# A filter bias written by ScalarE before the products, in place of a bias product behind them, in a two-layer graph kernel

## What is computed

```python
def layer0(features, edge_distances, ...):                 # bf2 is a filter bias
    h = features @ W_lin.T
    basis = gaussian_smearing(edge_distances)               # 50 columns
    ef = shifted_softplus(basis @ Wf1 + bf1) @ Wf2 + bf2    # the filter, 128 per edge
    messages = h[senders] * ef
    agg = segment_sum(messages, receivers)
    return shifted_softplus(agg @ Wm1 + bm1) @ Wm2 + bm2

def layer1(node_feats, edge_vec, edge_length, ...):         # mlp_b2 is a filter bias
    emb = radial_embedding(edge_length)                     # 8 columns
    h = silu(emb @ mlp_w0 + mlp_b0)
    h = silu(h @ mlp_w1 + mlp_b1)
    w = (h @ mlp_w2 + mlp_b2).reshape(-1, 4, 32)            # the filter
    # four products of w with the gathered features and the edge's direction,
    # then segment_sum per receiver and an output product

x = layernorm(x + layer0(x, edge_weight, ..., src, dst))
x = layernorm(x + layer1(x, edge_attr_3, edge_weight, src, dst, ...))
```

## Time and profile before

| | |
|---|---|
| time, median of 3 executions | 2209.0 us (2207.32 to 2209.87) |
| time of the profiled execution | 2202.79 us |
| span of the profiled execution | 2201.0 us |
| TensorE busy | 1899.1 us (86%) |
| VectorE busy | 1370.4 us (62%) |
| ScalarE busy | 637.9 us (29%) |
| GpSimd busy | 1569.6 us (71%) |
| mean granted TensorE clock | 0.823 of 2.4 GHz |

### The profile page before, as it was taken

The page is one execution under the profiler, slowest core; times in us unless marked ns, Lnnn a source line. Parts: engine busy times, 40 slices in busy tenths (PEclk is TensorE's granted clock), DMA queues, the critical chain, the costliest instruction groups (busy, mean ns, idle before and its releaser), DMA issues.

```text
span 2201.0 us, 34359 instructions
## 1 busy us (share of the span) xinstructions
PE 1899.1 (86%) x10138; PEld 1431.4 (65%) x10138; DVE 1370.4 (62%) x2905; ACT 637.9 (29%) x995; POOL 1569.6 (71%) x1599
## 2 busy tenths in 40 slices
PE   5887877778777887777879999999999999899997
PEld 4665666666666666666557777666776676677766
DVE  6755555555555555555645776666667666666665
ACT  3643343343433433432541111111111111111114
POOL 4777777777777777777147777777777777777770
PEclk8777777777777777777867998898999998988889
DMA  7422222222222222222021111111121221111112
GB/s 217 126 78 78 76 81 76 76 81 76 76 81 76 80 76 76 81 76 62 6 82 51 55 54 53 53 54 54 53 55 54 54 55 54 52 55 54 53 52 66
DMA packets 105683, 152.31 MB, mean 69 GB/s; under 512 B 33982, under 2 KB 65490, under 8 KB 105546
## 3 DMA queue, kind: packets, MB, share of 16 engines
q0 software_dynamic: 50656, 103.11, 17.3%
q1 hardware_dynamic: 54652, 46.76, 7.0%
q10 hardware_dynamic: 336, 2.01, 0.3%
HBM read 138.53 MB, written 13.21 MB: 69 GB/s over the span
## 4 chain that ended last, share of the span: by engine, by line
POOL 68%; issue 22%; PE 7%; DMA 1%; DVE 1%; ACT 1%; SPq 0%; POOLq 0%; DVEq 0%; ACTq 0%
POOL sent L436 68%; DMA unit_in<-in_x 1%; PE bank L984 1%; PE bank L800 1%; PE bank L767 1%; PE bank L815 1%; PE bank L953 1%; PE bank L759 1%; PE bank L988 0%; PE bank L942 0%; PE bank L871 0%; PE bank L879 0%; PE bank L802 0%; DMA sent<-up_table,senders 0%; DMA sent<-h_table,senders 0%
## 5 line engine op out<-in xcount | busy, mean ns | idle before, releaser
L436 POOL DMA_INDIRECT sent<-up_table,senders x784 | 775.3, 989 | 268.2 <-issue 237.7
L436 POOL DMA_INDIRECT sent<-h_table,senders x784 | 766.5, 978 | 263.9 <-issue 238.6
L815 PE MATMUL bank<-onehot,msg 128*128 128x128 f32 x4704 | 794.0, 332 | 7.1 <-DVE sums L1098 4.2
L815 PEld LDWEIGHTS bank<-onehot,msg 128*128 128x128 f32 x4704 | 706.4, 235 | 116.0 <-issue 91.4
L800 PE MATMUL bank<-Wf_sb,hid 128*128 128x128 f32 x1568 | 281.1, 334 | 94.8 <-DVE hid L1114 94.5
L1124 DVE TENSOR_TENSOR msg<-bank,sent 128x512 f32<-128x512 f32 x196 | 135.6, 692 | 349.1 <-issue 189.7
L800 PEld LDWEIGHTS bank<-Wf_sb,hid 128*128 128x128 f32 x1568 | 246.0, 239 | 153.5 <-DVE hid L1114 100.2
L800 PEld LDWEIGHTS bank<-w_sb,h 64*128 64x128 f32 x1568 | 195.5, 193 | 213.1 <-issue 116.2
L631 ACT ACTIVATE soft<-soft 128x512 f32<-128x512 f32 (+1 forms) x209 | 131.2, 628 | 591.2 <-DVE soft L1105 558.4
L1085 DVE TENSOR_TENSOR onehot<-relT,iota 128x512 f32<-128x512 f32 x392 | 268.8, 686 | 39.3 <-PE bank L815 37.1
L800 PE MATMUL bank<-w_sb,h 64*128 64x128 f32 x1568 | 233.9, 291 | 47.3 <-DVE msg L1157 46.4
(11 more groups left out here) (133 smaller groups left out, 1330.4 us busy)
## 6 DMA issues: line engine op xcount, KB each, us to landing
basis<-in_edge_weight SPq DMA_DIRECT2D x196, 100.0 KB
sent<-h_table,senders POOLq DMA_INDIRECT x784
sent<-up_table,senders POOLq DMA_INDIRECT x784, 2.5
basis<-near_lengths SPq DMA_DIRECT2D x196, 16.0 KB
radial_embedding<-basis SPq DMA_DIRECT2D x196, 16.0 KB
emb_in<-radial_embedding SPq DMA_DIRECT2D x98, 32.0 KB
unit_in<-in_x SPq DMA_DIRECT2D x12, 256.0 KB, 3.7
h_table<-h SPq DMA_DIRECT2D x12, 256.0 KB, 2.8
```

The costliest lines, as they stand in the source:

```text
L436: pool.indirect_dma_start(sent[:, n % SLOTS, j, :], None, table, bass.IndirectOffsetOnAxis(pick, 0))\
L815: last = t_.matmul(ps[:, k, :], msg[:, p, j, k * P:(k + 1) * P], onehot[:, p, j, :], start=(j == 0), stop=(j == HALF_CHUNKS - 1))
```

## The change

ScalarE gets a tile `bias_rows` (128 partitions x 3 x 128, each partition holding the three bias vectors), filled once: TensorE multiplies `ones_bf` by all of `bias3` into bank 7, ScalarE copies the result out. TensorE waits for that copy (`s_biases`) ahead of its flag read, ScalarE ahead of its loop.

In the loops ScalarE then copies one bias row, broadcast four times, into the whole filter bank of a half (`seed`), once the message of the half two back has been made from that bank. TensorE waits for this copy (`seeded`) in place of the message and does its four products with `start=False` onto what stands there; its bias product is gone, but for the first two halves of each layer, where it comes ahead of the four products with `start=True`. The dense stage still uses `products`.

```diff
+    bias_rows = sb("bias_rows", [P, 3, P])
...
+        def seed(sm, h, which):
+
+            if h.counter.eng is None and h.rel < 2:
+                return
+            b = h.before(2)
+            wait(act, sm["msg"], b.upto())
+            a.activation(filtB[h.parity], bias_rows[:, which:which + 1, :]
+                         .broadcast_to([P, HALF_CHUNKS, P]), ACT.Copy).then_inc(sm["seeded"], 1)
...
             if b.real():
                 soft_log(L0, b.parity, ("exped", "logged"), HALF, b.upto())
+                seed(L0, b, 0)
...
         act.wait_ge(s_weights, 1)
+        act.wait_ge(s_bias, 1)
+        a.activation(bias_rows[:, :, :].rearrange("p a b -> p (a b)"), bank[7][:, 0:3 * P],
+                     ACT.Copy).then_inc(s_biases, 1)
+        act.wait_ge(s_biases, 1)
         for_halves(act, iterations, layer0, 2)
...
+            b = h.before(2)
+            if b.real():
+                seed(L1, b, 2)
+        for_halves(act, iterations, layer1, 2)
...
+        def onto_bias(sm, h, lhs, weight, which):
+
+            out_bank = filtB[h.parity]
+            if h.counter.eng is None and h.rel < 2:
+                b = h.before(2)
+                wait(pe, sm["msg"], b.upto())
+                t_.matmul(out_bank, ones_bf[:, :],
+                          bias3[:, which:which + 1, :].broadcast_to([3, HALF_CHUNKS, P]),
+                          start=True, stop=False, skip_group_check=True)
+            else:
+                b = h.before(2)
+                wait(pe, sm["seeded"], b.upto())
+            for j in range(HALF_CHUNKS):
+                last = t_.matmul(out_bank[:, j, :], lhs(j), weight, start=False, stop=True,
+                                 skip_group_check=True)
+            last.then_inc(sm["filt"], 1)
...
         def filter0(h):
             p = h.parity
-            b = h.before(2)
-            wait(pe, L0["msg"], b.upto())
             wait(pe, L0["soft"], h.upto())
-            products(filtB[p], HALF_CHUNKS, P, lambda j: hid[:, p, j * P:(j + 1) * P],
-                     Wf2_sb[:], 0).then_inc(L0["filt"], 1)
+            onto_bias(L0, h, lambda j: hid[:, p, j * P:(j + 1) * P], Wf2_sb[:], 0)
...
         pe.wait_ge(d_bparts, 48)
+        pe.wait_ge(s_turned, 12)
+        t_.matmul(bank[7][:, 0:3 * P], ones_bf[:, :], bias3[:, :, :].rearrange("p a b -> p (a b)"),
+                  start=True, stop=True).then_inc(s_bias, 1)
+        pe.wait_ge(s_biases, 1)
```

More of the change, by code:

```diff
@@ L320, in build @@
     s_weights = sem("s_weights")
+    s_bias, s_biases = sem("s_bias"), sem("s_biases")
     s_flag, s_fits = sem("s_flag"), sem("s_fits")
@@ L349, in edge_sems @@
         return by_dma | {k: sem(f"L{layer}_{k}") for k in
-                         ("filt1", "filt", "msg", "window", "added") + own}
+                         ("filt1", "filt", "msg", "window", "added", "seeded") + own}
     L0, L1 = edge_sems(0), edge_sems(1)
@@ L702, in layer1 @@
                         .then_inc(L1["act2"], 1)
-        for_halves(act, iterations, layer1, 0)
+            b = h.before(2)
+            if b.real():
+                seed(L1, b, 2)
+        for_halves(act, iterations, layer1, 2)
         def finish(back):
@@ L883, in filter1 @@
             p, g = h.parity, h.pair_slot
-            b = h.before(2)
-            wait(pe, L1["msg"], b.upto())
             wait(pe, L1["act2"], h.pair_upto())
             rows = slice(p * HIDDEN, (p + 1) * HIDDEN)
-            products(filtB[p], HALF_CHUNKS, P, lambda j: h2[rows, g, j * P:(j + 1) * P],
-                     w2_sb[rows, :], 2).then_inc(L1["filt"], 1)
+            onto_bias(L1, h, lambda j: h2[rows, g, j * P:(j + 1) * P], w2_sb[rows, :], 2)
         def layer0(h):
```

## The result

The change made the kernel about 0.5% slower. Median of five executions 2217.55 us (2215.52 to 2222.16), against 2207.32 us (2205.17 to 2209.87, five) for the kernel before: ratio 1.0054, 95% interval 1.0037 to 1.0071.

What follows compares the result with a forecast made beforehand. GpSimd's successive gathers were taken as the bound. The profiled 2202.79 us less 1.4 at layer 1's start gave 2201.4; keeping the timed median's 6.2 us distance gave 2207.6 us, range 2198 to 2217.

Steps and rivals of the forecast that it cites:

- What queues behind a seed in layer 0: ScalarE in layer 0: next basis, Exp and Ln stand behind the seed; hidden product some 1.5 us later, 1.6 us spare, cost 0.
- The stretches: Gathers beginning just after a VectorE one-hot last longer, 62 us in all on the chain; how they would move couldn't be fixed.
- I take no shift for the forecast: Mean gather durations in both layers taken as unchanged; bounds from trace stretches were 20 us less and 18 us more.
- rival 2: Later filters and window sums move one-hots into gather starts: +5 us in layer 1, +6.5 in layer 0, 2219 us; chance 0.20.
- Half of these ends for the range: Range 2198 to 2217: the forecast less 10 and plus 9 us, half of the bounds on longer or shorter gathers.
- The bias products worth nothing on the chain: TensorE, steady part of both layers: 388 products removed, 170 us of busy time, beside the gathers, so worth nothing.
- Seeds: ScalarE's 388 copies into PSUM, taken at 0.63 us each, 244 us more busy time, hidden.
- Waits in layer 1: TensorE's filter in layer 1 waits some 0.8 us longer for a seed where it had caught up; cost 0.
- The start of layer 1: GpSimd's message waits there shrink: first by 1.06 us, second's excess of 0.34 us goes; gain 1.4 us, between 0 and 3.5.
- The way into layer 0: Setup product and copy ahead of the first basis; first hidden product near 52.5 instead of 51.01; cost 0, at most 3 us.
- Rival 3: TensorE's granted clock falls to 0.77 in layer 1 and it becomes the bound: 13 us, 2221 us; chance 0.05.

## Why the prediction was wrong

It said 2207.6 us, no change the likeliest, in a range of 2198 to 2217; measured 2217.55, just outside the range and slower.

- **The step that failed** is "What queues behind a seed in layer 0 ... Cost 0". Its picture was right: the basis behind the seed, the hidden product later (1.3 us, where it said 1.5), TensorE able to take it, GpSimd never short of a message. But it asked only whether somebody would *wait*. What followed the late hidden product was not followed to its end: SyncE's distance loads wait for that product too. They start some 1.6 to 1.9 us later behind the gathers, by the table, and later loads alone make the kernel 0.4% slower (2213.33 us against 2204.85); the change makes it 0.54% slower. I had not looked at that queue. A part of the rest, as four one-hot buffers show, went by the late window sums, which the step had at nothing too. In a kernel in which a gather's duration hangs on what VectorE does in 0.1 us, cover is not enough; the phase has a price too.
- **The stretches.** "I take no shift for the forecast" was the second half of the same error. The bounds were right in kind, and rival 2 named the mechanism (one-hots moved into a gather's start), with 0.20. It put +5 us in layer 1 and +6.5 in layer 0; measured in the profiles +1.9 and +18.5. That its total of 2219 us lies near the measured one is partly luck, for the places were wrong. Its way was wrong in part: the one-hots of most stretched gathers do not hang on late window sums (8 of the 82 had waited for them), and without those waits the mean is still 992 ns. "Half of these ends for the range" had no ground: one place that changes in every iteration moves 49 iterations together, so the phases don't average out, and the end itself was the honest bound. Layer 0 was bounded with 0.995, a mean of one window of layer 1; in the profiled execution it reached 1.001. The 62 us of stretches that it read from the means were a good measure of what they cost, but only 51 of them (25.0 and 26.4 us in the two layers) lie behind one-hots; 8 lie behind `dots`. One-input one-hots on the kernel before saved 50.5 us of the median (2206.8 to 2156.26).
- **The bias products worth nothing on the chain:** right, shown by the version without them, 1.0001. TensorE lost 228 us of busy time, more than the 170 forecast. The higher clock of this profile, below, can account for the rest.
- **Seeds:** 601 ns each against 630 taken. ScalarE's busy time rose by 208 us, though its seeds sum to 233.3: rows of ScalarE overlap a little (a seed at 558.66 for 0.60, the basis at 559.20). Sixteen bias products of 512 columns are left; I said 17.
- **Waits in layer 1:** TensorE's filter waits 113.7 us for seeds where it waited 47.3, and it costs nothing, as forecast; seeds in layer 1 alone give 0.9994.
- **The start of layer 1:** GpSimd's waits for messages went from 4.4 us (three) to 1.9 (one). The forecast of 1.4 us counted what exceeds the usual gap of 0.30; counted in this way the gain is 3.5 - 1.6 = 1.9 us. The second wait is gone, as forecast, and the first lost 1.55 us where 1.06 was forecast. The same window that the earlier trace rows came from:

```profile
1184.32 1.38 POOL L438 DMA_INDIRECT sent<-up_table,senders  x1 [0.30 <-issue]
1187.59 0.94 POOL L438 DMA_INDIRECT sent<-up_table,senders  x1 [1.89 <-DVE msg L1191]
```

- **The way into layer 0:** cost 0, right. The first hidden product starts at 51.51 in place of 51.01, 1.0 us before the 52.5 forecast, and the first message at 60.35, earlier than before. The timeline:

```profile
49.37 0.49 ACT L661 ACTIVATE bias_rows<-bank 128x384 f32<-128x384 f32 x1 [9.43 <-PE bank L963]
49.89 0.72 ACT L623 ACTIVATE basis<-basis,neg_centers 122x512 f32<-122x512 f32 x1
...
51.51 2.08 PE L888 MATMUL bank<-basis,Wf_sb 50*128 50x256 f32 x8 [2.24 <-ACT basis L626]
```

- **Rival 3, a falling clock:** the clock did not fall. The same three stretches as in the earlier trace rows, each with the granted clock third from the end:

```profile
400.00:600.00 200.00, 124.06 (x767) 107.76 (x765) 111.48 (x191) 98.18 (x152) 153.07 (x155) 0.83 0.26 76
1200.00:1400.00 200.00, 174.82 (x1034) 133.43 (x1034) 137.47 (x316) 49.20 (x80) 153.69 (x153) 0.93 0.19 53
1600.00:1800.00 200.00, 178.26 (x1008) 138.73 (x1006) 135.28 (x310) 46.93 (x76) 153.07 (x155) 0.89 0.19 54
```

TensorE is less busy in all three, and the clock rose from 0.77 to 0.83 in layer 0 and stayed near 0.9 in layer 1. The mean of the whole is 0.857 where it was 0.823, but other executions of the kernel before had 0.822 to 0.854, so only part of that rise is the change's. In both traces the clock switches between its two levels, 1.2 and 2.4 GHz: between 150 and 1040 us it has 47 stretches at 1.2 GHz before and 64 after, while the time at 1.2 GHz in the whole kernel went from 782 us to 635. The Trainium skill (TensorE: Matmul & The Clock Gate, A second HAM failure mode) says that short idle times between groups make the clock oscillate. The trace agrees that it does, and more often in layer 0 with the longer waits, but the mean did not fall by it.

What the prediction said would show it did show it: the layer's length changed with the mean of its gathers, so it is the stretches, and no message of layer 0 was late.

## What to carry to other kernels

When an added wait is "hidden", follow everything that is released by the delayed work to its last reader, the DMA queues too, and ask for each not only whether someone waits, but what it will now run beside. In a hardware loop such a shift is the same in every iteration: take the far bound for the range, not half. And where the bounding engine's own instruction has two durations, remove the cause (here the VectorE instruction with two SBUF inputs that both layers have, 2.3 to 2.6%) before tuning anything beside it. Put a wait behind the work that others need early, not ahead of it: the same seeds one place later cost nothing.

## What the runs showed of the hardware

- A gather's issue on GpSimd takes 0.94 us, and up to 1.47 when it begins within some 0.5 us *after* the start of a one-hot with two SBUF inputs. The order matters to a tenth: a gather that began 0.18 us before the one-hot (557.50 and 557.68, above) took 0.94, one 0.08 us after it (557.68, 557.60) took 1.43. Nearer than 0.05 us either can win. Here, in the changed kernel, the gather did, and the one-hot took 0.74 us in place of 0.68:

```profile
556.61 0.74 DVE L1119 TENSOR_TENSOR onehot<-relT,iota 128x512 f32<-128x512 f32 x1 [1.26 <-PE bank L851]
556.62 0.94 POOL L438 DMA_INDIRECT sent<-h_table,senders  x1 [0.30 <-issue]
```

- Whatever the distance, a stretched gather ends some 1.50 us after the one-hot's start (1.43 us long from 0.08 behind it, 1.24 from 0.26 behind it). It is as if the gather could begin only 0.56 us into the 0.69 of the one-hot. Behind the 0.56 us of `dots` the end is some 1.37 us after its start (1.28 long from 0.09 behind it), so as if from 0.43 on. A one-hot that begins while a gather is under way lengthens neither of them, as at 557.68.
- What stretches a gather is an instruction with two inputs in SBUF, and not any instruction of VectorE: in the traces of before and after each of the gathers over 1.0 us from 150 us on begins up to 0.55 us behind the start of a one-hot, `dots<-sent,dirT` or `msg<-msg,dirT`, while the 35 gathers of layer 0 before that begin 0.05 to 0.5 us behind the start of `msg<-bank,sent`, which has one input in PSUM, take 0.94 to 0.95. This agrees in kind with the Trainium skill (GPSIMD Engine Reference, 1. Specifications); the size and the dependence on who starts first are from these rows.
- The one-input form, four instructions of 308 ns in place of one of 686, leaves the gathers at 947 and 949 ns: between 150 and 1040 us none takes over 1.2 us.
- A stretched gather carries its stretch on: its rows land later by as much, the message and the next one-hot with them, and that one-hot again meets a gather. A small load of distances that starts up to 1.0 us behind the gather makes the message later by some 0.5 to 0.6 us more and breaks this. A transfer that makes gathered rows later can thus make the kernel faster.
- ScalarE writes 128x512 of fp32 into PSUM in 601 ns; the same-size copy out of PSUM took 598.
